# The inverse deviation of the layer norms as a power on GpSimd

## The reference

```
x = x + 0.5 * ffn(layernorm(x))
x = x + attention(layernorm(x))
x = x + 0.5 * ffn(layernorm(x))

layernorm(x) = (x - mean(x)) / sqrt(var(x) + 1e-5)      # over the 128 columns

attention: q, k, v = x @ W.T + b; for each of 4 tiles of 128 keys a softmax of its own
           over its 128 scores; the four outputs added, divided by (sum of all weights + 1e-6); @ Wo.T + bo

ffn: scores = x @ router (8 experts); the 2 highest per token; gate = sigmoid(score)
     routed: for each chosen expert e: h = silu((g x) @ w_in[e]) * ((g x) @ w_sw[e]); out += h @ w_out[e]
     shared: (silu(x @ w_in_sh.T) * (x @ w_sw_sh.T)) @ w_out_sh.T
```

## Time and profile before

| | |
|---|---|
| median of the runs | 1123.97 us |
| span of the profiled execution | 1269.8 us |
| TensorE (PE) busy | 963.1 us, 76% |
| VectorE (DVE) busy | 733.0 us, 58% |
| GpSimd (POOL) busy | 657.6 us, 52% |
| ScalarE (ACT) busy | 632.5 us, 50% |
| mean granted TensorE clock | 0.897 of full |

### The profile page before, as it was taken

The page is one execution under the profiler, slowest core; times in us unless marked ns, Lnnn a source line. Parts: engine busy times, 40 slices in busy tenths (PEclk is TensorE's granted clock), DMA queues, the critical chain, the costliest instruction groups (busy, mean ns, idle before and its releaser), DMA issues. The chain is left out here.

```text
span 1269.8 us, 22393 instructions
## 1 busy us (share of the span) xinstructions
PE 963.1 (76%) x5226; PEld 710.5 (56%) x5227; DVE 733.0 (58%) x2844; ACT 632.5 (50%) x1836; POOL 657.6 (52%) x922
## 2 busy tenths in 40 slices
PE   3767766198888897489979788973388888887798
PEld 2565645176666676245545454542266666665676
DVE  3775655355555454267877787866155545544576
ACT  4545553044444454378867576761144444443332
POOL 1666655456666666300555455466466666656122
PEclk9778786699999999699988898995599999999899
DMA  7311111222222222211211110011222222221354
GB/s 204 100 41 43 44 40 36 61 62 71 71 68 71 71 66 65 77 33 34 62 40 60 39 55 28 23 34 41 61 68 72 69 68 72 70 68 56 88 164 146
DMA packets 114444, 83.78 MB, mean 66 GB/s; under 512 B 15202, under 2 KB 105444, under 8 KB 114404
## 3 DMA queue, kind: packets, MB, share of 16 engines
q1 hardware_dynamic: 95808, 47.89, 14.1%
q0 software_dynamic: 16896, 34.77, 8.2%
q10 hardware_dynamic: 1700, 0.66, 0.2%
HBM read 42.74 MB, written 40.51 MB: 66 GB/s over the span
## 5 line engine op out<-in xcount | busy, mean ns | idle before, releaser
L628 POOL DMA_INDIRECT pairs<-PAY,POS x256 | 256.6, 1002 | 83.4 <-issue 83.4
L827 POOL DMA_INDIRECT results<-arena x272 | 268.2, 986 | 56.5 <-POOL spare_p L267 36.8
L895 PE MATMUL bank<-WOE,HT 128*128 x1088 | 180.7, 289 | 69.8 <-issue 40.4
L895 PEld LDWEIGHTS bank<-WOE,HT 128*128 128x128 f32 x1088 | 143.0, 190 | 147.9 <-issue 147.0
L858 ACT ACTIVATE HT<-bank 128x256 f32<-128x256 f32 x272 | 104.3, 383 | 184.7 <-PE bank L901 115.1
L267 POOL TENSOR_TENSOR spare_p<-spare_p 1x1 f32<-1x1 f32 x304 | 59.4, 195 | 242.7 <-DVE arena L811 155.8
L805 DVE TENSOR_TENSOR H<-bank,SG 128x256 f32<-128x256 f32 x272 | 115.4, 424 | 99.8 <-ACT SG L854 58.2
L816 DVE TENSOR_TENSOR XSL<-bank,XSH 128x128 fp32r<-128x128 f32 x272 | 79.1, 291 | 148.8 <-ACT XSH L862 111.7
L854 ACT ACTIVATE SG<-bank 128x256 f32<-128x256 f32 x272 | 104.8, 385 | 78.6 <-PE bank L884 51.4
L882 PE MATMUL bank<-WEH,XSL 128*128 x272 | 131.8, 485 | 5.9 <-DVE XSL L816 3.8
L906 PE MATMUL bank<-ident,arena 128*128 128x128 f32 x272 | 75.6, 278 | 58.3 <-DMA arena<-pairs 57.3
(11 more groups left out here) (154 smaller groups left out, 1938.6 us busy)
## 6 DMA issues: line engine op xcount, KB each, us to landing
arena<-pairs SPq DMA_DIRECT2D x272, 64.5 KB
Y<-results SPq DMA_DIRECT2D x64, 256.0 KB
results<-arena POOLq DMA_INDIRECT x272
X<-L_attn_batch SPq DMA_DIRECT2D x16, 256.0 KB
pairs<-PAY,POS POOLq DMA_INDIRECT x256
out<-X SPq DMA_DIRECT2D x16, 256.0 KB, 3.1
pairs<-pad_rows SPq DMA_DIRECT2D x16, 64.5 KB
big<-L_ffn_w_in_eDF SPq DMA_DIRECT2D x1, 1024.0 KB, 5.5
```

What stands on the lines that cost most here:

```text
L628: pool.indirect_dma_start(pairs, bass.IndirectOffsetOnAxis(ap=POS[:, b.buf, j, c:c + 1], axis=0), PAY[:, b.buf, c, j, :], None).then_inc(s ...
L827: pool.indirect_dma_start(results, bass.IndirectOffsetOnAxis(ap=XS[:, t.buf, D:D + 1].bitcast(U32), axis=0), YO[:, t.buf, :], None).then_i ...
L895: mm = pe.matmul(bank[6 + od.buf % 2][:, 0:D], HT[:, od.buf % 2, c * P:(c + 1) * P], WOE[:, ds(e * FC * D + c * D, D)], start=(c == 0), st ...
```

## The change

SD, eps_c and the square root on ScalarE go, and so does the small Silu at the end of each body of stage 2. VectorE adds epsilon to the variance (tile VE) right after bn_aggr, behind a wait for its own bn_aggr, and only then signals. GpSimd raises VE to the power -0.5 (an elementwise operation against a tile minus_half) into RST and signals. `dve_rstd` issues nothing any more; it names the signal that the norm then waits for. In stage 2 the power for `ahead` stands in front of the scatters of `b`, and GpSimd's loop now begins two bodies earlier. In stage 4 the powers for `upd` and then `ahead` are the last things of GpSimd's body. `dve_norm` of stage 2 waits for the second half of PAY of the block two before.

```diff
--- before.py
+++ after.py
@@ -165,7 +165,7 @@
         pad_rows = sb("pad_rows", [P, E, ROW])
         pad_at = sb("pad_at", [1, E], I32)
         next_row = sb("next_row", [P, E])
-        eps_c = sb("eps_c", [P, 1])
+        minus_half = sb("minus_half", [P, BT])
         ints = sb("ints", [P, E * 2], I32)
 
         tile_no = sb("tile_no", [1, NT])
@@ -182,7 +182,7 @@
         XT32 = sb("XT32", [P, 2, W])
         ST = sb("ST", [P, 2, BT, 6])
         MV = sb("MV", [P, 2, BT, 2])
-        SD = sb("SD", [P, 2, BT])
+        VE = sb("VE", [P, 2, BT])
         RST = sb("RST", [P, 2, BT])
         SC = sb("SC", [P, BT, E])
         TOP = sb("TOP", [P, 2, BT, 8])
@@ -282,7 +282,6 @@
         wst = view(0, 6, D)
         spare_v = sb("spare_v", [1, 5])
         spare_p = sb("spare_p", [1, 3])
-        spare_a = sb("spare_a", [P, 1])
         vec_at = []
         stage = big[:, :, :, :].rearrange("p a b w -> p (a b w)")
 
@@ -328,7 +327,7 @@
             @block.gpsimd
             def _(pool):
                 st = Steps(pool, pool_s)
-                for m, v in ((ident, 0.0), (before, 1.0), (ones, 1.0), (eps_c, EPS), (spare_p, 0.0), (pad_rows, 0.0),
+                for m, v in ((ident, 0.0), (before, 1.0), (ones, 1.0), (minus_half, -0.5), (spare_p, 0.0), (pad_rows, 0.0),
                              (upto, 1.0)):
                     st.did(pool.memset(m[tuple(slice(None) for _ in m.shape)], v))
 
@@ -528,20 +527,21 @@
             carry(dve, 3 + which)
             for j in range(BT):
                 ins = dve.bn_aggr(MV[:, which, j, :], ST[:, which, j, :])
-            st.signals(ins, k[name], done + b.i + 1)
-
-        def act_std(act, b, which, stats, name, done):
-            act.wait_ge(k[stats], done + b.i + 1)
-            act.activation(SD[:, which, :], MV[:, which, :, 1], ACT.Sqrt, bias=eps_c[:, :]).then_inc(k[name], 1)
+            st.did(ins)
+            st.settle()
+            st.signals(dve.tensor_scalar(VE[:, which, :], MV[:, which, :, 1], EPS, None, ALU.add), k[name],
+                       done + b.i + 1)
+
+        def pool_rstd(pool, b, which, stats, name, done):
+            pool.wait_ge(k[stats], done + b.i + 1)
+            pool.tensor_tensor(RST[:, which, :], VE[:, which, :], minus_half[:, :], ALU.pow).then_inc(k[name], 1)
 
         def dve_rstd(dve, st, b, which, name, done):
-            dve.wait_ge(k[name], done + b.i + 1)
-            st.did(dve.reciprocal(RST[:, which, :], SD[:, which, :]))
-            return st.mark()
+            return k[name], done + b.i + 1
 
         def dve_norm(dve, st, b, done):
             n = done + b.i
-            if done:
+            if done or due(n - 1):
                 dve.wait_ge(k["pay1"], n - 1)
             for j in range(BT):
                 t = BT * b.i + j
@@ -741,10 +741,7 @@
                         act_high(act, new)
                     if b.live:
                         act_payload(act, b, 0)
-                    if ahead.live:
-                        act_std(act, ahead, 1, "r_stats", "r_std", 0)
-
-                    act.activation(spare_a[:, :], eps_c[:, :], ACT.Silu)
+
                     if isinstance(b.i, int) and b.i == -1:
 
                         act.wait_ge(k["weights_loaded"], 48)
@@ -769,7 +766,13 @@
 
             @block.gpsimd
             def _(pool):
-                rolled(pool, NB, 0, 0, lambda at: pool_scatter(pool, at(0), 0))
+                def body(at):
+                    ahead, b = at(2), at(0)
+                    if ahead.live:
+                        pool_rstd(pool, ahead, 1, "r_stats", "r_std", 0)
+                    if b.live:
+                        pool_scatter(pool, b, 0)
+                rolled(pool, NB, 2, 0, body)
                 for s in scattered:
                     pool.wait_ge(s, BT * TOPK * 16 * NB // 2)
 
@@ -1137,10 +1140,6 @@
                         act.wait_ge(k["k_made"], new.i + 1)
                         act.activation(KT, bank[5][:, :], ACT.Identity, bias=bk_s[:, :]).then_inc(k["k_ready"], 1)
 
-                    if ahead.live:
-                        act_std(act, ahead, 0, "a_stats", "a_std", 0)
-                    if upd.live:
-                        act_std(act, upd, 1, "r_stats", "r_std", NB)
                     if old.live:
                         act_gates(act, old, NB)
                     if c.live:
@@ -1245,7 +1244,7 @@
             @block.gpsimd
             def _(pool):
                 def body(at):
-                    ahead, old, out = at(2), at(-3), at(-4)
+                    ahead, upd, old, out = at(2), at(-2), at(-3), at(-4)
                     if ahead.live:
                         pool_sum(pool, ahead, 0)
                     if out.live:
@@ -1261,6 +1260,10 @@
 
                         pool.wait_ge(k["xt_copied"], NB + old.i + 1)
                         pool.tensor_copy(cut(XTR, W * old.i, W), XT32[:, old.buf, :]).then_inc(k["xt_split"], 1)
+                    if upd.live:
+                        pool_rstd(pool, upd, 1, "r_stats", "r_std", NB)
+                    if ahead.live:
+                        pool_rstd(pool, ahead, 0, "a_stats", "a_std", 0)
                 rolled(pool, NB, 2, 4, body)
                 for s in scattered:
                     pool.wait_ge(s, BT * TOPK * 16 * NB)
```

## The result

The changed kernel takes 1195.5 us, median of 4 runs (1193.7 to 1196.6), where the kernel before takes 1123.8. The ratio is 1.063, 95% interval [1.062, 1.065]: 72 us slower. Forecast was slower, but 1152 us, and 1195.5 lies above the range.

What follows compares the result with a forecast made beforehand. No engine is busy over 76%; TensorE (PE) bounds an attention body, and GpSimd's queue would after the change. Ring 18, end of stage 6, first stage 4: 28 us on 1124, so 1152 us, range 1124 to 1185.

Steps and rivals of the forecast that it cites:

- the ring: Attention: norm, GATE, PAY, scatters, copy, powers, next norm wait in a circle; 19.2 us a body, 18 us in all.
- the table loads: ScalarE: 68 loads, 87 us, go; hidden behind other waits in attention, so costed at 0.
- I take 0.5 us: GpSimd: assumed time of one power of 128x4, with ends 0.2 and 1.3 us.
- 38 us for each us: Whole kernel: forecast time grows about 38 us per us of a power's length; 0.2 gives 1141, 1.3 gives 1182.
- I let a little over half of it through, 4 us: First routing: GpSimd nearly the bound, so a little over half of 0.5 us in some 14 blocks costs 4 us.
- VectorE's part of the ring: Attention: from the start of the norm to the end of GATE, 4.0 us of the 19.2 us ring.
- bodies of 17 to 18 us: Attention in timed runs: body length taken as 17.5 us, so the ring adds 1.7 us in each of nine bodies.
- The end of the stage: Attention's last bodies: norm waits for a power behind the scatters, 13.7 us a body becomes 15.7, 6 us in all.
- I summed 5 us on the profiled span: Whole kernel, with stretched bodies: 3 for the ring, 6 at the stage's end, less 4 in the first stage.
- The rival of the slack: Attention: timed bodies over 19.2 us, as profiled, so only the end of the stage counts; 1129 us, chance 0.22.
- The faster rival: End of ScalarE's attention body: table loads were on the path, removing them gains time; 1108 us, chance 0.09.
- the dear first call: GpSimd: by the Trainium skill, a new operation's first call costs about 6 us, making the sum 6 us more.

Runs made afterwards that it cites:

- add_for_pow: The changed kernel with an addition in place of the power on GpSimd, same tiles and same place in its queue: 1165.1 us, ratio 1.038.
- idle_power_b: The kernel before with 48 powers added on GpSimd that nobody reads or waits for, in a set where the kernel before takes 1126.4 us: 1150.1 us, ratio 1.020.
- idle_power: The kernel before with 48 unread powers added on GpSimd, in a set where the kernel before takes 1268.7 us: 1269.8 us, ratio 1.002.
- no_sqrt: The kernel before with Identity for the square root on ScalarE and without the one-column Silu, so 68 table loads go: 1123.5 us, ratio 0.9996.
- base0: The kernel before, unchanged, profiled once more: 1121.9 us, profiled span 1120.0 us.
- mid4_att: The changed kernel with powers in the attention stage alone, before the last four scatters: 1246.0 us, ratio 0.978 (kernel before 1268.7); repeated in another set, 1138.5 us, ratio 1.010.

## Why the prediction was wrong

The mechanism was right in the main: GpSimd's work in the first routing, the ring in the attention stage, the wait behind the scatters at its end, and nothing for the table loads. All four stand in the traces, and the first two and the last are shown by runs as well. The sizes were off, all one way: 28 us forecast, 72 measured. One piece of the mechanism was missing, the norms that slow down beside GpSimd's sum.

- **"I take 0.5 us"** is the step that failed first. The power takes 1.04 to 1.06 us. At the prediction's own 38 us for each us (36 measured, add_for_pow) this is 21 of the missing 44 us. The end of the range, 1.3 us, held the price, and at 1.05 us the same sum would have said 1173: the rest of the miss is not the price.
- **"I let a little over half of it through, 4 us"** (first routing): 16 to 18 us. I weighed GpSimd's 11.0 us against VectorE's 10.1 and still gave it room; in an undisturbed execution a block is 10.25 us with GpSimd not waiting between blocks, and idle_power_b shows every power paid, together with the longer scatter. Beyond the price, some 6 us.
- **VectorE's part of the ring, "where nothing holds it up", 4.0 us**: 4.8 to 5.0. Read off bodies in which GpSimd's sum ran at another time; in the rows of the closed ring it starts with the norms. 10 bodies by 0.9: 9 us, an estimate from the length of the norms (1.9 to 2.05 us against 1.1). The wording "where nothing holds it up" hid that closing the ring fixes what runs beside what.
- **"bodies of 17 to 18 us", 17.5 taken**: 17.1, and 10 of them count. Some 4 us.
- **The end of the stage, 3 x 2.0 = 6 us**: 13.3 over five bodies. The base of 13.7 us a body came from the stretched trace and is 12.4; my 15.7 for after becomes the measured 16.2 with the dearer power. Beyond the price 6 us. With the price, 21, and the 6, 9 and 4 before, this makes 46 for the missing 44 us: the account closes to 2 us.
- **Reading past the stretch** was right, and the timed runs bear it out: I summed 5 us on the profiled span and took 28, because one body written out ran at 17 us. The rival of the slack might have held had all executions been like the profiled one: there the powers as work cost nothing (idle_power, ratio 1.002), but the whole change was not run there. But I held to the stretched trace where I should have left it too: for the blocks of the first routing and the end of the stage.
- **The table loads**: cost 0, and measured 0 (no_sqrt). The faster rival falls, and so does the dear first call: the first power starts 0.1 us after VE is ready (18.54 us against 18.45) and takes 1.05 us, and the longest of the 48 takes 1.5. The Trainium skill (ScalarE: Activation LUTs, What ACT_TABLE_LOAD costs) would have made the loads twice as dear; by the trace they are not, and off the path either price is worth nothing.

## What to carry to other kernels

Moving a small operation to an engine with a long queue can cost more by its place in that queue than by its length (here 41 us against 31): ask what stands ahead of it, who waits for it, and whether that waiter feeds the queue again; if so, walk the ring once and compare it with the body. Where an engine is idle for no time between two blocks, expect every added microsecond to be paid in full, whatever its busy share over the whole span (52% in the first profile, 59% in base0). And when the profiled span is far over the timed runs, take no slack from it: profile once more before believing that something is covered.

## What the runs showed that I had not expected

- A power of 128x4 on GpSimd takes 1.06 us, an addition of the same tiles 0.22 us: nearly five times.
- VectorE's 128x128 operations with per-row scalars slow down beside a 128x512 operation of GpSimd: four norms 1.1 us alone and 1.9 to 2.4 beside a sum, four products 1.66 to 2.70.
- The same kernel runs in 1124 to 1126 us in most sets of runs and in 1269 us in one, and its first profiled execution was of the long kind. The long set ran on another chip than the three experiment sets beside it; whether the chip is the cause was not tested. In it the code in rolled loops is stretched most (bodies of 21 to 24 us against 17, where the two bodies written out ran at 17 to 19), in all stages. mid4_att is faster there by 2% while slower by 1% elsewhere. What stretches it is not settled.
